# A recommendation tower on one core: a weight sum moved behind product copies, table splits in pieces, one gathered unit and one MLP step moved

## What is computed

```python
e = jnp.stack([tbl_0[ids[:, 0]], ..., tbl_25[ids[:, 25]]], axis=1)          # 2048 x 26 x 128
sd = jnp.einsum('bfd,bd->bf', e, dense)
ss = jnp.einsum('bfd,bgd->bfg', e, e)
z = jnp.concatenate([dense, sd, ss[:, iu, ju]], axis=1)                     # iu < ju
h = jnp.concatenate([z, dense], axis=1)
h = jnp.maximum(h @ W_top1 + b_top1, 0.0)
h = jnp.maximum(h @ W_top2 + b_top2, 0.0)
y = h @ W_top3
```

## Time and profile before

| | |
|---|---|
| median of 3 runs | 361.9 us (360.82 to 363.86) |
| the profiled execution | 359.05 us, its span 357.1 us |
| PE busy | 335.2 us, 94% |
| PEld busy | 286.4 us, 80% |
| POOL busy | 241.8 us, 68%; the 236 gathers 241.3 us |
| DVE busy | 206.6 us, 58% |
| ACT busy | 204.0 us, 57% |
| a lookup of 16 matmuls on PE, in the chain | 3.65 us |
| PE's granted clock | full in the whole span |
| DMA | 40.93 MB, mean 115 GB/s, 199 GB/s in the first 60 us |

### The profile page before, as it was taken

How to read it: one execution, slowest core, us unless ns; L and a number is a source line. 1 busy time by engine, 2 the same in 40 slices (tenths; PEclk the granted TensorE clock), 3 DMA queues, 4 the chain that set the end, 5 groups by cost and what they waited for, 6 DMA issues and landing times.

```text
span 357.1 us, 8260 instructions
## 1 busy us (share of the span) xinstructions
PE 335.2 (94%) x3388; PEld 286.4 (80%) x3388; DVE 206.6 (58%) x486; ACT 204.0 (57%) x267; POOL 241.8 (68%) x242
## 2 busy tenths in 40 slices
PE   0799999697999999999999999999999999999996
PEld 0677777586988888888998888898898888898885
DVE  0889898565328874628328886527427787145111
ACT  3378897484736575763663664872572666664111
POOL 6777777777777777777777777777777777720000
PEclk9999999999999999999999999999999999999999
DMA  6999729536355225254247243246236321124400
GB/s 154 241 261 250 194 61 269 148 93 164 76 143 138 65 69 132 55 127 124 53 108 183 75 105 84 68 95 155 59 83 177 100 64 48 51 51 121 113 24 1
DMA packets 46342, 40.93 MB, mean 115 GB/s; under 512 B 29039, under 2 KB 40423, under 8 KB 46306
## 3 DMA queue, kind: packets, MB, share of 16 engines
q1 hardware_dynamic: 38754, 24.94, 27.4%
q0 software_dynamic: 7552, 15.48, 17.3%
HBM read 34.64 MB, written 5.76 MB: 113 GB/s over the span
## 4 chain that ended last, share of the span: by engine, by line
PE 77%; POOL 8%; DMA 5%; issue 4%; DVE 3%; SPq 2%; ACT 1%; DVEq 0%
PE oh_ps L538 34%; PE dot_ps L556 15%; PE mlp_ps L574 15%; POOL rows L367 8%; PE mlp_ps L583 7%; PE tr_ps L522 7%; DMA rows<-tbl_dram,idx_sb 3%; DVE onehot L462 2%; DMA b_sb<-b_top_dram 2%; ACT feat L391 1%; DMA idx_sb<-idx_dram 0%; SPq L320 0%; SPq L316 0%; SPq L319 0%; DVE h L481 0%
## 5 line engine op out<-in xcount | busy, mean ns | idle before, releaser
L367 POOL DMA_INDIRECT rows<-tbl_dram,idx_sb x236 | 241.3, 1023 | 73.3 <-issue 70.7
L462 DVE TENSOR_SCALAR onehot<-ids_bc 125x512 fp32r<-125x512 int16 x360 | 142.4, 448 | 33.2 <-PE oh_ps L538 19.1
L538 PE MATMUL oh_ps<-onehot,table_hi 125*128 125x512 f32 x360 | 115.5, 402 | 12.0 <-DVE onehot L462 11.9
L538 PE MATMUL oh_ps<-onehot,table_lo 125*128 125x512 f32 x360 | 111.7, 392 | 0.0
L399 ACT ACTIVATE feat<-oh_ps 128x512 f32<-128x512 f32 x45 | 54.7, 1217 | 62.8 <-PE oh_ps L538 61.7
L391 ACT ACTIVATE feat<-tr_ps 128x512 f32<-128x512 f32 x59 | 73.0, 1241 | 26.3 <-PE tr_ps L522 25.8
L538 PEld LDWEIGHTS oh_ps<-onehot,table_hi 125*128 125x128 f32 x360 | 65.6, 190 | 24.4 <-issue 12.8
L538 PEld LDWEIGHTS oh_ps<-onehot,table_lo 125*128 125x128 f32 x360 | 68.1, 189 | 14.8
L556 PE MATMUL dot_ps<-feat 128*54 128x52 f32 x2048 | 57.8, 214 | 5.7 <-ACT feat L391 1.8
L556 PEld LDWEIGHTS dot_ps<-feat 128*54 128x54 f32 x2048 | 54.5, 130 | 10.1 <-issue 6.1
L471 DVE COPY dots<-dot_ps 54x416 f32<-54x416 f32 x56 | 33.2, 594 | 36.2 <-PE dot_ps L556 34.9
(11 more groups left out here) (24 smaller groups left out, 65.4 us busy)
## 6 DMA issues: line engine op xcount, KB each, us to landing
ids_bc<-ids_t_dram SPq DMA_DIRECT2D x45, 128.0 KB, 3.9
dots_scratch<-dots SPq DMA_DIRECT2D x28, 175.5 KB
rows<-tbl_dram,idx_sb POOLq DMA_INDIRECT x236
dots<-tbl_dram SPq DMA_DIRECT2D x6, 480.0 KB
w_sb<-tbl_dram SPq DMA_DIRECT2D x3, 480.0 KB
zt<-dots_scratch SPq DMA_DIRECT2D x12, 117.0 KB
dense_sb<-dense_f_dram SPq DMA_DIRECT2D x8, 128.0 KB, 2.6
zt<-tbl_dram SPq DMA_DIRECT2D x2, 480.0 KB
```

What stands on the lines that cost most here:

```text
L367: nc.gpsimd.indirect_dma_start(rows[:, i % RING, k, t, :], None, tables[f], bass.IndirectOffsetOnAxis(ap=idx_sb[:, j % 2, x:x + 1], axis=0 ...
L462: last = nc.vector.tensor_scalar(onehot_part(m, part)[:, c, :], ids_bc[0:TP, m % IDSLOTS, :], float(part * PROWS + c), None, ALU.is_equal)
L538: last = nc.tensor.matmul(oh_ps[:, m % 2, :], table[0:TP, u, row * D:(row + 1) * D], onehot_part(m, part)[:, c, :], start=(table is table_ ...
```

## The change

1. In FIRST, `r9` moves from before `j0 l11 c11` to behind it.
2. In LAST, `r14` is taken out. TAIL does the same unit as `q14`, behind `k2 k3` and ahead of the product groups `d0` to `d7`; `k3` moves from behind `d7` to that place.
3. `split_lo` makes the low part of a table in four pieces of 256 columns instead of one of 1024, each ahead of the one-hot part that is multiplied with it. PE waits for the piece that it needs. SP's waits on `lo_made` count pieces.
4. The sum of the two weight blocks moves on DVE from behind the last table's one-hot parts to behind the product copies of chunk 0. With it moves its wait for all weight DMAs.

```diff
-         "l6 c6 s8 i8 r5 l7 c7 s9 i9 r6 f l8 c8 s10 i10 l9 c9 s11 i11 r8 l10 c10 r9 j0 l11 c11 e0 e1 e2 e3 r10 j1 "
+         "l6 c6 s8 i8 r5 l7 c7 s9 i9 r6 f l8 c8 s10 i10 l9 c9 s11 i11 r8 l10 c10 j0 l11 c11 r9 e0 e1 e2 e3 r10 j1 "
...
-        "m0 m1 r12 e0 e1 e2 e3 r13 e4 e5 e6 e7 r14")
-TAIL = "k2 d0 d1 d2 d3 d4 d5 d6 d7 k3 k4 o0 o1 o2 o3 o4 m0 m1 m2 m3 m4"
+        "m0 m1 r12 e0 e1 e2 e3 r13 e4 e5 e6 e7")
+TAIL = "k2 k3 q14 d0 d1 d2 d3 d4 d5 d6 d7 k4 o0 o1 o2 o3 o4 m0 m1 m2 m3 m4"
...
-                    sp.wait_ge(lo_made, u - RAWS + 1)
+                    sp.wait_ge(lo_made, PARTS * (u - RAWS + 1))
...
-            sp.wait_ge(lo_made, RAWS)
+            sp.wait_ge(lo_made, PARTS * RAWS)
...
-            def split_lo(u):
+            def split_lo(u, part):
+
                 dve.wait_ge(hi_made, u + 1)
-                nc.vector.tensor_tensor(table_lo[0:TP, u, :], raw_table(u)[0:TP],
-                                        table_hi[0:TP, u, :].bitcast(fp32), ALU.subtract).then_inc(lo_made, 1)
+                cs = slice(part * PROWS * D, (part + 1) * PROWS * D)
+                nc.vector.tensor_tensor(table_lo[0:TP, u, cs], raw_table(u)[0:TP, cs],
+                                        table_hi[0:TP, u, cs].bitcast(fp32), ALU.subtract).then_inc(lo_made, 1)
...
             for u in range(NO + 1):
-                split_lo(u)
                 for part in range(PARTS):
+                    split_lo(u, part)
                     make_part(u, part)
-            dve.wait_ge(weights_loaded, WEIGHT_DMAS * DMA)
-            nc.vector.tensor_tensor(w1_sb[:, ZC, :], w1_sb[:, ZC, :], w1_dense2, ALU.add).then_inc(w1_summed, 1)
...
                 dots_to_sbuf(n)
-                if 0 < j < NPAIR - 1:
+                if j == 0:
+                    dve.wait_ge(weights_loaded, WEIGHT_DMAS * DMA)
+                    nc.vector.tensor_tensor(w1_sb[:, ZC, :], w1_sb[:, ZC, :], w1_dense2, ALU.add
+                                            ).then_inc(w1_summed, 1)
+                elif j < NPAIR - 1:
                     layer3(n - 1)
...
                 if j == 0:
                     pe.wait_ge(hi_made, u + 1)
-                    pe.wait_ge(lo_made, u + 1)
...
                 for part in range(PARTS):
+                    if j == 0:
+                        pe.wait_ge(lo_made, PARTS * u + part + 1)
                     pe.wait_ge(onehot_made, PARTS * m + part + 1)
```

## The result

The changed kernel takes 358.63 us in the median of 10 runs (357.67 to 359.60), the kernel before 361.63 in 10 runs (359.81 to 363.86). The ratio is 0.9917, with a 95% interval from 0.9893 to 0.9942: 3.0 us or 0.8% faster, within the 1% that was called no change. The forecast was 360.9, range 358.0 to 363.9; the sign and the range held, the gain was three times the one forecast. The spread of the runs fell from 4.0 to 1.9 us, which turns out to matter.

The account below looks back on a forecast made before the run. PE is busiest, but POOL's gathers hold it to their pace at units 28 and 43. Terms: -2.6 (smaller of X and G) + 1.4 + 0.2 = -1.0 us, 358.0 profiled, plus 2.9 is 360.9; range 358.0 to 363.9.

Parts of the forecast that it names:

- min(X, G): At unit 28, where PE and POOL arrive together, PE keeps only the smaller of X and G: 2.6 us.
- X: What PE wins before unit 28, up to e0 and at the weight blocks' sum: 3.1 us, between 2.2 and 3.8.
- G: What POOL wins as gathers meet short pieces instead of long table splits: 2.6 us, bounds 0 or slightly below and 3.9.
- I take 1.3: First pair of chunks: pieces and r9's move let the last lookup l11 end 1.3 us earlier, a part of X.
- only six overlaps of twelve cost anything: Gathers beside table splits: the argument given for rival 1, that the mechanism behind G isn't seen in each overlap.
- rival 1: Gathers lose as much to 48 short pieces as to 12 long ones, G = 0: 1.6 us slower, 363.5; chance 0.17.
- All 1.77 us goes.: First product groups: with the sum moved behind the copies, PE's whole 1.77 us gap there vanishes, a part of X.
- That distance I carry over.: The runs' median, 361.9, lies 2.9 us above the profiled time; the same 2.9 was added to the forecast 358.0.
- r9, 1.1 us within X: Moving r9 behind l11 saves its 0.69 us wait and 0.44 us of transposes, if DVE lets l11 start earlier.
- The tail costs 1.4 + 0.2: Last chunk: d0 waits 1.4 us for the last unit's ACT copy, m0 0.2 us for the last reload.
- rival 3: DVE becomes the bound, needing 0.6 us a table more; X = 1.8, a gain of 0.2 us, 361.7; chance 0.15.
- rival 2: Ordinary runs wait at r14, the last unit, so the new tail gains up to 3.46 us: 358.3 and below; chance 0.18.

Follow-up runs that it names:

- e7: e4 without the pieces, tables split in one piece each: 359.11 us, ratio 0.9934 to the kernel before.
- e4: The changed kernel with LAST and TAIL of the kernel before (r14 and k3 at their old places): 357.06 us, ratio 0.9884 to the kernel before.
- e2: The kernel before with only the low parts made in four pieces: 361.18 us, ratio 0.9983 to the kernel before.
- e1: The kernel before with only the sum of the weight blocks moved behind the first product copies: 359.43 us, ratio 0.9957.
- e11: e5 with r9 at its old place and, in SECOND, q13 ahead of l1: 357.27 us, ratio 0.9888 to the kernel before, on another chip than e5.
- e10: e4 with a table's four pieces made one behind the other, ahead of its one-hot parts: 357.88 us, ratio 0.9895 to the kernel before, on another chip.
- e8: The kernel before, sum at its old place but waiting on its own semaphore for only the two blocks it adds: 358.56 us, ratio 0.9926.
- e3: The kernel before with only the tail changed, r14 taken out and TAIL starting k2 k3 q14 d0: 362.71 us, ratio 1.0033.
- e6: e4 with r9 back before `j0 l11 c11`: 357.05 us, ratio 0.9880 to the kernel before.
- e5: The changed kernel with TAIL starting k2 q14 k3 d0 in place of k2 k3 q14 d0: 356.92 us, ratio 0.9873 to the kernel before.

## Why the prediction was right in sign, and where its sizes were off

- **PE and POOL in step, min(X, G).** Right as a mechanism. e7 (X without G) lost 2 us to e4, e2 (G without X) won 0.6 where e4's combination won 4.2, and e1, e7 and e11 have the waits for rows at the units 13, 24 and 28. The gates were a little softer than forecast, as units 43 and 58 never bound again: after the change unit 43 is used 1.1 us after it lands. The size was off: in the profiled execution unit 28 lets 1.4 us pass, where min(X, G) was put at 2.6, as X was 2.4 and the rows took 4.0 us to land, not 3.52. With the tail's 1.6 us that makes +0.2, and the profiled executions differ by +0.5, not by the forecast -1.0.
- **"I take 1.3", what the pieces and r9 win before e0.** Mis-sized: e0 starts 0.6 us earlier. It is the prediction's other case, 0.5 to 0.8 us if the units 4 and 5 land no earlier: unit 5 was used at 42.58 as before.
- **G = 2.6 us, from gathers that meet a table split.** Right, 2.5 in the trace; e10 and e7 tie it to the length of the DVE instruction. The mechanism can be seen more sharply than the prediction had it: what counts is whether a gather starts inside a split. The earlier trace rows have one that does, and it ends 0.82 us after the split (47.13 and 46.31). So do the other four long ones of that trace, by 0.81 to 0.82 us, and one that starts 0.13 us ahead of a split takes its 0.94. So "only six overlaps of twelve cost anything" speaks for the mechanism and not for rival 1.
- **"All 1.77 us goes."** Right as a mechanism, and of the profiled execution it is right in size too (2.4 us at the first lookup less 0.6 at e0). For the median it was sized too small: 1.77 was one execution's value. Other traces of the old place have 2.8 and 3.8 us, as the last weight lands between 65.1 and 66.2 us and PE may be earlier. e8 shows that the landing is most of the cost.
- **"That distance I carry over."** This is the step that failed. The 2.9 us between the profiled execution and the median were taken as a constant, and the change removes them: after it the profiled run lies 0.9 us above the median. In part they were that same wait, longer in other executions, and the half clock behind it: 48 of 63 runs of the kernel before had a lower mean clock and none of the changed kernel's. The prediction doesn't mention the clock, and its trace had no sign of it. A reader of the trace alone should have asked why ordinary runs of before were 1 to 5 us slower than the profile. That the median came inside the range, though the profiled executions went the other way, is luck in this sense: what the forecast left out had the right sign.
- **The spread.** The kernels that keep the old sum or the long splits spread by 2.8 us or more (e1, e2, e3, e7, e8); with both replaced it is 0.6 to 1.6 us in the experiments, with six runs or fewer each, and 1.9 in the changed kernel's ten runs.
- **r9, 1.1 us within X.** Wrong in the total: e6 shows 0.0. The step said "if DVE lets l11 start earlier". DVE doesn't let it end earlier.
- **The tail costs 1.4 + 0.2.** Right: 1.27 + 0.3 in the trace, 1.6 by e4, 1.2 by e3 (1.27 + 0 in its trace). That it buys nothing was right as well (at its old place unit 58 is used 1.8 us after it lands in e4).
- **DVE as the bound (rival 3).** Four pieces take 1.35 us in e10 where one split takes 1.13, so the price was +0.2 us a table, not rival 3's +0.6. The Trainium skill gives a fixed cost per instruction (VectorE: DVE Perf Modes, the section on the TRN2 errata), by which the prediction estimated +0.5. Its durations hold (0.41 to 0.42 us for 256 columns, 0.424 by its formula), but the starts lie 0.34 us apart.
- **Rival 1** (no gain on POOL) is out by the 2.5 us, **rival 2** (the last gate in ordinary runs) by e3, which was slower and not faster. Its sign was a gain over 3 us, and the measured 3.0 reaches it: the gain had another source, as above.
- **What the profile was to show.** Of the signs of being right, no gap of 1.8 us in e0 to e7, no gather above 1.4 us, POOL's end at 313.3 and the wait at d0 (1.27) came. The second pair began at 72.90 and not near 72.2, and PE waited 1.1 us at unit 28 (its loader 1.51), not 0.3 to 0.7.

On why a gather waits, the Trainium skill (SBUF — State Buffer, the section on its two separate sides) says that a Vector instruction with two inputs in SBUF holds, until it ends, a port that a GpSimd instruction which reads SBUF needs. The 1.88 and 1.89 us of e7 beside splits of 1.2 us, and at most 1.19 in the changed kernel beside pieces of 0.41, agree; no run separates that port from another cause. Which other DVE instructions a gather waits for is in the last section.

The best kernels seen with all their work are e4, e5 and e6, 356.9 to 357.1, 1.2 to 1.3% faster than the kernel before and 1.6 to 1.7 us faster than the changed one. Between them the runs don't decide.

## What to carry to other kernels

When two engines run in step, cost every early gain as the smaller of what each wins, and expect that two edits which win little alone can pay together. Before a term is read from one trace, ask whether the wait ends in a DMA landing: another execution can pay twice the price (3.83 us for 1.77 here), and a profiled run faster than the timed ones is a sign of it. Compare the mean granted clock of the timed runs with the profiled one's before taking the profile for the usual case. Give a wait only the DMAs that it needs, and put a piece of independent work between a transpose and the product that reads its copy.

## What the runs showed of the hardware that was not expected

A gather's length depends on which DVE instruction is running when it starts. Inside a two-input split of 1.2 us it took up to 1.89 us (1.97 in e1) and ended 0.81 to 0.86 us after the split. Of the 98 that started inside a one-hot in the kernel before, which has only one input, 79 ended 0.80 to 0.86 us after it too. Eight that started within 0.03 us of the one-hot's own start took the 0.94 of a gather alone. Inside a copy that reads the products' results from PSUM it took 0.94, as alone, in all 24 cases of the kernel before, though up to 0.58 us of the copy were left. One of them, timeline of the kernel before (DVE and POOL):

```profile
69.68 0.59 DVE L471 COPY dots<-dot_ps 54x416 f32<-54x416 f32 x1 [0.69 <-PE dot_ps L556]
69.89 0.94 POOL L367 DMA_INDIRECT rows<-tbl_dram,idx_sb  x1 [0.30 <-issue]
```

So it isn't every busy stretch of DVE that costs POOL time. Twelve splits at the start decided 2 us of a 357 us kernel (e7 against e4). Over the whole kernel before, the 236 gathers take 241.3 us where 236 of 0.94 would take 222: 19 us of POOL's time, an estimate from these two numbers, still go to what runs beside it, mostly one-hots.

PE's granted clock fell to half for 3.4 us after PE had stood 3.83 us (e2), and 48 of 63 timed runs of the kernel before have a mean clock of 0.989 to 0.995, where that execution has 0.995.

Rows of unit 5 landed 8.6 us after the last gather was issued in the changed kernel and 7.2 before: they landed at the same time though issued 1.4 us earlier, in a stretch where the DMA engines were 79% to 81% busy. There an earlier issue bought nothing.
